# Second attention of a two-layer kernel: keys cut as three tiles of 128 and a rest of 16 instead of four tiles of 100

## The reference, cut to what matters

```
q = (dst @ Wq.T).reshape(B, T_q, H, D_K)          # B 4, T_q 512 here, H 16, D_K 16
k = (src @ Wk.T).reshape(B, T_k, H, D_K)
v = (src @ Wv.T).reshape(B, T_k, H, D_K)
scores = jnp.einsum('bqhd,bkhd->bhqk', q, k)
scores = scores + bias[None]
scores = jnp.where(mask, scores, -1000000000.0)
attn = jax.nn.softmax(scores, axis=-1)
out = jnp.einsum('bhqk,bkhd->bqhd', attn, v).reshape(B, T_q, H * D_K)
return out @ Wo.T
```

## Time and profile before

| | |
|---|---|
| median of 3 runs | 666.35 us |
| profiled execution | 666.83 us, of which the span is 665.0 us |
| TensorE busy | 615.3 us (93%) |
| VectorE / ScalarE / GpSimd busy | 341.1 / 263.4 / 122.0 us |
| chain that ended last | PE 76%, DVE 12%, DMA 4%, issue 3%, ACT 2% |
| mean granted TensorE clock | 0.982 |

### The profile page before, as it was taken

One profiled execution on the slowest core, in us unless ns is written; L12 is line 12 of the kernel. 1 busy time (PEld: TensorE's weight loads), 2 busy tenths in 40 slices (PEclk: granted clock), 3 DMA queues, 4 the chain that ended last, 5 costly groups with the idle time before them and its releaser, 6 DMA issues.

```text
span 665.0 us, 9145 instructions
## 1 busy us (share of the span) xinstructions
PE 615.3 (93%) x3054; PEld 376.6 (57%) x3055; DVE 341.1 (51%) x1089; ACT 263.4 (40%) x364; POOL 122.0 (18%) x178
## 2 busy tenths in 40 slices
PE   3999999999999668799999879999999999999998
PEld 1666666666666435699998433334334333436665
DVE  4264442301303687232232967687887887834301
ACT  0211111111111333334442356776676667683321
POOL 0000000000002000256551036230040040043410
PEclk9999998998989899899999889999999999999999
DMA  9993600811400613253324794252552400041141
GB/s 314 358 366 113 215 1 2 294 61 63 131 0 1 226 54 100 91 139 104 111 71 124 198 155 75 28 86 50 95 86 47 92 1 2 2 131 46 40 135 64
DMA packets 51208, 71.05 MB, mean 107 GB/s; under 512 B 7632, under 2 KB 39802, under 8 KB 50762
## 3 DMA queue, kind: packets, MB, share of 16 engines
q1 hardware_dynamic: 49114, 64.98, 35.7%
q0 software_dynamic: 2048, 5.51, 2.9%
HBM read 48.74 MB, written 15.13 MB: 96 GB/s over the span
## 4 chain that ended last, share of the span: by engine, by line
PE 76%; DVE 12%; DMA 4%; issue 3%; ACT 2%; POOL 1%; DVEq 0%; POOLq 0%; ACTq 0%; SPq 0%
PE ps L955 13%; PE ps L971 13%; PE ps L1536 8%; PE ps L1518 6%; PE ps L1425 6%; PE ps L1143 5%; PE ps L1151 4%; PE ps L1262 4%; PE ps L1274 3%; DVE arena L2265 3%; DVE arena L1976 3%; PE ps L1187 2%; PE ps L1448 2%; PE ps L941 1%; PE ps L1236 1%
## 5 line engine op out<-in xcount | busy, mean ns | idle before, releaser
L1769 ACT ACTIVATE arena<-ps 100x1024 f32<-100x1024 f32 x128 | 123.8, 1020 | 54.7 <-PE ps L1518 54.5
L2265 DVE TENSOR_REDUCE arena<-ps 128x1 f32<-128x400 f32 x256 | 129.5, 563 | 27.7 <-PE ps L1425 25.9
L1576 ACT ACTIVATE arena<-ps 128x512 f32<-128x512 f32 x50 | 29.9, 597 | 172.3 <-PE ps L955 160.5
L955 PE MATMUL ps<-xnT,arena 128*128 128x512 f32 x192 | 94.6, 619 | 0.9 <-DVE xnT L1834 0.9
L971 PEld LDWEIGHTS ps<-arena 128*128 128x128 f32 x384 | 74.1, 194 | 32.2 <-issue 24.3
L971 PE MATMUL ps<-arena 128*128 128x256 f32 x384 | 92.0, 384 | 0.0
L1425 PE MATMUL ps<-arena 97*128 97x400 bf16 x256 | 75.2, 338 | 3.8 <-DMA arena<-arena 1.9
L1518 PE MATMUL ps<-arena 100*100 100x512 bf16 x256 | 76.2, 381 | 1.9 <-DMA arena<-arena 0.7
L1536 PE MATMUL ps<-arena 100*32 100x512 f32 x512 | 69.1, 604 | 0.0
L1425 PEld LDWEIGHTS ps<-arena 97*128 97x128 bf16 x256 | 20.2, 97 | 74.3 <-DVE arena L2265 47.5
L955 PEld LDWEIGHTS ps<-xnT,arena 128*128 128x128 f32 x192 | 37.1, 197 | 29.5 <-issue 27.5
(11 more groups left out here) (247 smaller groups left out, 718.8 us busy)
## 6 DMA issues: line engine op xcount, KB each, us to landing
arena<-in_W SPq DMA_DIRECT2D x16, 512.0 KB, 9.7
arena<-in_ctxT SPq DMA_DIRECT2D x4, 1664.0 KB, 7.4
arena<-in_ctxN SPq DMA_DIRECT2D x4, 1664.0 KB, 12.0
arena<-arena SPq DMA_DIRECT2D x48, 128.0 KB
last_k_parts<-arena SPq DMA_DIRECT2D x24, 100.0 KB, 1.8
arena<-last_k_parts SPq DMA_DIRECT2D x8, 300.0 KB
x_tok<-in_x SPq DMA_DIRECT2D x4, 512.0 KB, 9.3
xn_rows<-xn SPq DMA_DIRECT2D x4, 512.0 KB
```

Source lines behind the costliest of these rows:

```text
L955: ins = pe.matmul(ps[:, 4 + k % 2, :], ctxT_s[:, b % 2, c, f * P:f * P + P], xnT[:, c, S * b:S * b + S], start=(c == 0), stop=(c == KC - 1))
L1576: act.activation(hid[:, k % 4, :], ps[:, 4 + k % 2, :], ACT.Gelu_apprx_tanh).then_inc(s_a, 1)
L1769: act.activation(pexp2[0:KT, c % 4, :, :], ps[0:KT, 2 + 2 * (c % 2):4 + 2 * (c % 2), :], ACT.Exp).then_inc(f_pe, 1)
L2265: dve.tensor_reduce(nm2[:, m // MU % 2, h, j:j + 1], ps[:, FAST.bank(x), 0:KF], AX.X, ALU.max, negate=True).then_inc(s_by["dve"], 1)
```

## The change

- The 400 keys are cut in three tiles of 128 and a rest of 16 keys. Step t = 3 treats the rest: the four heads' scores go as four matmuls with 32 stationary columns each (the last 32 keys, of which the first 16 belong to tile 2) into the four 32-row quarters of one bank. One exponential of 128x512 takes them. Values of the rest are laid out in a tile that is zero outside the block of each head and outside the 16 keys, so that one 128x128 matmul of two instructions adds all four heads' rests.
- A unit has 7 exponentials instead of 8 (`OWN_EXPS`).
- Values of the rest are made by eight matmuls of four strips instead of two; ScalarE copies that piece with one instruction and four small ones, scaled by a column of zeros and ones (`C_REST`). GpSimd prepares the tile with further small instructions. The stored values of batches 2 and 3 have 128 rows instead of 100.
- The maxima products are dealt as 5, 5, 4 and 2 to the four steps (`MAXIMA_IN`), and `LEAD` is 28.
- The turned maxima stand at the beginning of step t = 2, on TensorE ahead of its scores and on ScalarE ahead of its exponentials (`first_of_step`). VectorE's own split for unit 1 moves from step 1 to step 0.

TensorE in one unit without extras, before: L1536 are the values, L1425 maxima products, L1518 scores, L1438 the turned maxima. The piece runs from the values made in the unit's step 0 to the turned maxima in its step 2.

The diff, cut to its core:

```diff
+FULL_T = KF // P
+RK = KF - FULL_T * P
+assert CT == FULL_T + 1 and RK == 16
...
-LEAD = 26
+LEAD = 28
+OWN_EXPS = 2 * FULL_T + 1
+MAXIMA_IN = (0, 5, 10, 14, 16)
...
+    rest = (np.arange(P)[:, None] % VW >= VW - RK).astype(np.float32)
...
+def first_of_step(st):
+    u, t = divmod(st, CT)
+    return [("max rows", u + 1)] if t == 2 and u + 1 < UNITS else []
...
-    if t == 2 and u + 1 < UNITS:
-        found.append(("max rows", u + 1))
...
-def maxima_of_step(st, lo, hi):
-    first = LEAD + HG * st
-    return range(min(first + lo, UNITS * MU), min(first + hi, UNITS * MU))
+def maxima_of_step(st, lo, hi=None):
+    u, t = divmod(st, CT)
+    first, end = LEAD + MU * u + MAXIMA_IN[t], LEAD + MU * u + MAXIMA_IN[t + 1]
+    hi = end if hi is None else first + hi
+    return range(min(first + lo, UNITS * MU), min(hi, UNITS * MU))
+
+
+def exps_from(st):
+
+    u, t = divmod(st, CT)
+    return OWN_EXPS * u + 2 * t
+
+
+def step_of_exp(c):
+    u, r = divmod(c, OWN_EXPS)
+    return CT * u + r // 2
...
     for st in range(STEPS):
+        for name in first_of_step(st):
+            yield name, next(turns), TAKER[name[0]]
         for m in maxima_of_step(st, 0, 2):
             yield ("max", m), next(turns), TAKER["max"]
         for name in extras(st):
             yield name, next(turns), TAKER[name[0]]
-        for m in maxima_of_step(st, 2, HG):
+        for m in maxima_of_step(st, 2):
...
-                            ins = pe.matmul(bank[0:KT, t * D:t * D + D], ctx_e[:, b, k, tt * KT:tt * KT + KT], wv[:, k, :],
-                                            start=(k == 0), stop=(k == KC - 1), skip_group_check=True)
+                        if tt < FULL_T:
+                            for k in range(KC):
+                                ins = pe.matmul(bank[:, t * D:t * D + D], ctx_e[:, b, k, tt * P:tt * P + P], wv[:, k, :],
+                                                start=(k == 0), stop=(k == KC - 1), skip_group_check=True)
+                        else:
+                            for k in range(KC):
+                                for j in range(HG):
+                                    ins = pe.matmul(bank[VW * j:VW * j + VW, t * D:t * D + D], ctx_e[:, b, k, KF - VW:KF], wv[:, k, :],
+                                                    start=(k == 0), stop=(k == KC - 1), skip_group_check=True, tile_position=(0, VW * j))
...
-                assert LEAD == MU + 10
+                assert LEAD == MU + 12
                 queries(2, lambda i: max_products(range(MU + 2 + 2 * i, MU + 4 + 2 * i)))
+                max_products(range(MU + 10, LEAD))
                 pe.wait_ge(s_qf, KC * 2)
...
+                        for x in first_of_step(st):
+                            make(x)
                         for hp in range(HG // 2):
-                            c = 2 * st + hp
-                            if c >= 2:
-                                pe.wait_ge(f_pe, c - 1)
-                            for j in range(2):
-                                h = g * HG + hp * 2 + j
-                                ins = pe.matmul(ps[0:KT, 2 + 2 * (c % 2) + j, :], K2[0:KROWS, b % 2, h, t * KT:t * KT + KT], Q2[0:KROWS, b % 2, h, :],
-                                                start=True, stop=True)
-                            ins.then_inc(s_st, 1)
+                            c = exps_from(st) + hp
+                            if t < FULL_T or hp == 0:
+                                if c >= 2:
+                                    pe.wait_ge(f_pe, c - 1)
+                                for j in range(2) if t < FULL_T else range(HG):
+                                    h = g * HG + hp * 2 + j
+                                    if t < FULL_T:
+                                        ins = pe.matmul(ps[:, 2 + 2 * (c % 2) + j, :], K2[0:KROWS, b % 2, h, t * P:t * P + P], Q2[0:KROWS, b % 2, h, :],
+                                                        start=True, stop=True)
+                                    else:
+                                        ins = pe.matmul(ps[VW * j:VW * j + VW, 2 + 2 * (c % 2), :],
+                                                        K2[0:KROWS, b % 2, h, KF - VW:KF],
+                                                        Q2[0:KROWS, b % 2, h, :], start=True, stop=True, tile_position=(0, VW * j))
+                                ins.then_inc(s_st, 1)
                             max_products(maxima_of_step(st, hp, hp + 1))
                         for x in extras(st):
                             make(x)
                     if st >= 1:
                         i, tv = divmod(st - 1, CT)
                         bv = i // NG
-                        c = 2 * (st - 1)
+                        c = exps_from(st - 1)
                         if tv == 0 and i % NG == 0 and bv >= 2:
                             pe.wait_ge(f_v[bv % 2], 16)
-                        pe.wait_ge(f_pe, c + 2)
+                        pe.wait_ge(f_pe, exps_from(st))
                         if tv == 0 and i >= 1:
                             pe.wait_ge(f_oc, i)
                         if tv == 0 and i == 0:
                             taken(FAST, ("queries", 2, 1))
-                        for j in range(HG):
-                            ins = pe.matmul(ps[VW * j:VW * j + VW, 6, :], V2[0:KT, bv % 2, tv, i % NG * HG + j, :],
-                                            pexp2[0:KT, (c + j // 2) % 4, j % 2, :],
-                                            start=(tv == 0), stop=(tv == CT - 1), tile_position=(0, VW * j))
+                        if tv < FULL_T:
+                            for j in range(HG):
+                                ins = pe.matmul(ps[VW * j:VW * j + VW, 6, :], V2[:, bv % 2, tv, i % NG * HG + j, :],
+                                                pexp2[:, (c + j // 2) % 4, j % 2, :], start=(tv == 0), stop=False, skip_group_check=True,
+                                                tile_position=(0, VW * j))
+                        else:
+                            ins = pe.matmul(ps[:, 6, :], V2[:, bv % 2, tv, i % NG * HG:i % NG * HG + HG, :].rearrange("p h v -> p (h v)"),
+                                            pexp2[:, c % 4, 0, :], start=False, stop=True, skip_group_check=True)
                         ins.then_inc(f_pv, 1)
                     if st < STEPS:
-                        max_products(maxima_of_step(st, 2, HG))
+                        max_products(maxima_of_step(st, 2))
...
-                    act.wait_ge(s_evi, b // 2 + 1)
-                    t = 2 * (u - KC)
-                    act.activation((V2 if b < 2 else vst)[0:KT, b % 2, t:t + 2, :, 0:DK],
-                                   bank[0:KT, :].rearrange("p (t h d) -> p t h d", t=2, d=DK), ACT.Copy).then_inc(s_ev, 1)
+                    act.wait_ge(s_evi, (HG + 1) * (b // 2 + 1))
+                    v = (V2 if b < 2 else vst)[:, b % 2, :, :, 0:DK]
+                    found = bank[:, :].rearrange("p (t h d) -> p t h d", t=2, d=DK)
+                    if u == KC:
+                        ins = act.activation(v[:, 0:2, :, :], found, ACT.Copy)
+                    else:
+                        act.activation(v[:, 2, :, :], found[:, 0, :, :], ACT.Copy)
+                        for j in range(HG):
+                            lo = VW * j
+                            ins = act.activation(v[lo:lo + VW, FULL_T, j:H:HG, :], found[lo:lo + VW, 1, j:H:HG, :], ACT.Copy, scale=cst[lo:lo + VW, C_REST:C_REST + 1])
...
-                    for hp in range(HG // 2):
-                        c = 2 * st + hp
+                    for x in first_of_step(st):
+                        take_max_rows(x[1])
+                    for c in range(exps_from(st), exps_from(st + 1)):
                         act.wait_ge(s_st, c + 1)
                         if c >= 4:
-                            act.wait_ge(f_pv, (c - 4) // 2 + 1)
-                        act.activation(pexp2[0:KT, c % 4, :, :], ps[0:KT, 2 + 2 * (c % 2):4 + 2 * (c % 2), :], ACT.Exp).then_inc(f_pe, 1)
+                            act.wait_ge(f_pv, step_of_exp(c - 4) + 1)
+                        if st % CT < FULL_T:
+                            act.activation(pexp2[:, c % 4, :, :], ps[:, 2 + 2 * (c % 2):4 + 2 * (c % 2), :], ACT.Exp).then_inc(f_pe, 1)
+                        else:
+                            act.activation(pexp2[:, c % 4, 0, :], ps[:, 2 + 2 * (c % 2), :], ACT.Exp).then_inc(f_pe, 1)
                     for x in extras(st):
-                        if x[0] == "max rows":
-                            take_max_rows(x[1])
...
-                    max_steps(maxima_of_step(st, 2, HG))
-                    if t == 1 and 1 <= u + 1 < OWN_SPLITS:
+                    max_steps(maxima_of_step(st, 2))
+                    if t == 0 and 1 <= u + 1 < OWN_SPLITS:
                         split_maxima(u + 1)
...
-            for v in (V2, vst):
-                pool.memset(v[:, :, :, :, DK + 1:], 0.0)
```

(12 more changed lines are left out.)

15 lines of the change are left out of this document (8 added, 7 removed).

## The result

The changed kernel takes a median of 674.11 us (667.79 to 681.64, 11 runs) beside 666.68 us (665.5 to 670.26, 11 runs) of the kernel before, measured together. Two of the changed kernel's executions, 678.03 us and the profiled one, were in a slower state with a lower granted clock, and the ratios in this document leave such executions out: 1.0092 here (95% interval 1.0062 to 1.0123), which is the median of the other nine, 672.84 us, over 666.68. So the change costs 6.2 us by those nine and 7.4 by all eleven. The forecast was 673.8 us, slower.

The account below looks back on a forecast made before the run. TensorE's issue was taken to bound the loop, VectorE two microseconds behind. Units 5.5 + 1.0 + 0.7 + 0.7 + 1.3, tail -2.6 and search +0.9 gave +7.5 on 666.35: 673.8 us, range 657 to 680 (the forecast's own 669 to 680).

Parts of the forecast that it names:

- Work removed: TensorE in a unit: rest's scores 0.45 instead of 0.87, its values 0.87 instead of 1.00, 0.09 less to enter.
- the unit's own issue: TensorE in a unit without extras: 10.40 us, the 11.48 worked out less 1.08 of waits.
- The prices of going into strips and out: TensorE, changing between full-width and strip matmuls: 0.09 us going in and 0.14 going out, explained by a drain.
- one after the other: Rival: the rest's four score matmuls don't overlap in step 3, 0.42 us more per unit, 680 us; chance 0.06.
- Waits added: TensorE waits for banks, 0.54 before step 1's first product and 0.50 before the turned maxima: unit without extras +0.69.
- without waits: Rival: reductions free banks in time, thirteen units take 10.40 instead of 10.79, 659.5 us, 655 without drains; chance 0.16.
- half of them: Rival: waits overlap old ones and strips cost less, +0.2 per unit, about 667 us, 664 without drains; chance 0.20.
- The other units: Loop units walked singly: u4, u8 +1.0; u5, u9 +0.6; u6, u10 +0.5; u7, u11 +0.7; two batches 5.5.
- The tail: u14 and u15, no bank waits and the turned maxima's copy earlier: -2.6 us, of which 1.2 and 1.4.
- The search: Stage before the loop: four small value copies and strip matmuls lengthen the chain, +0.9 us (0.2 to 1.4).
- u0: First of the loop's sixteen units: change 0, as ScalarE is late anyway and two more products are done beforehand.
- The clock: TensorE might lose full clock with a tenth of the loop idle; given nothing of its own, windows showing 1.00.

Follow-up runs that it names:

- half_reduction: Changed kernel, but VectorE's maxima reduction reads only 200 of the 400 columns, leaving out half the keys: 660.29 us, ratio 0.9912.
- keys_only: Kernel before with only the new key tiles: parts 4, 4, 4, 4, lead 26, turned maxima behind step 2's scores, split in step 1: 661.35 us, ratio 0.9920.
- spread: Changed kernel, but in steps 0 and 1 the third maxima product stands ahead of the values, so never three in a row: 668.64 us, ratio 1.0039.
- mask_gpsimd: Changed kernel, but ScalarE copies each value piece in one instruction and GpSimd multiplies the rest's tile by a mask: 673.70 us, ratio 1.0118.
- lead_only: Changed kernel, but four products in each step and turned maxima behind step 2's scores; lead 28 and split in step 0 kept: 663.95 us, ratio 0.9965.
- late_turn: Changed kernel, but turned maxima back behind step 2's scores; parts 5, 5, 4, 2 and lead 28 kept: 668.55 us, ratio 1.0035.
- own_split_late: Changed kernel, but VectorE's split for unit 1 moved back from step 0 to step 1: 676.27 us, ratio 1.0182.
- even_parts: Changed kernel, but parts of 4, 4, 4, 4; turned maxima still first in step 2, lead 28: 669.28 us, ratio 1.0023.
- parts_only: Changed kernel, but lead 26, turned maxima behind step 2's scores and split in step 1; parts 5, 5, 4, 2 kept: 671.31 us, ratio 1.0080.
- tail_early: keys_only with the turned maxima first in step 2 only from u13 on: 662.89 us, ratio 0.9957.
- both: keys_only with turned maxima first from u13 on and GpSimd's mask in place of the four small copies: 662.21 us, ratio 0.9962.
- order_only: Kernel before with its four tiles of 100 and all the rest of the change (parts 5, 5, 4, 2, lead 28, turned maxima first): 683.80 us, ratio 1.0240.

## Why the prediction was right, and where it was not

**Work removed, and the unit's own issue.** 10.40 was worked out, and half_reduction's 10.91 less its 0.5 of waits is 10.4. (The 10.45 of keys_only is another sum: its turned maxima stand directly ahead of the values, where they cost 0.24 and not the 0.42 that they cost ahead of scores, and some 0.3 of small waits is left in it.) The prices of going into strips and out, taken from the earlier trace rows, therefore hold; the rest's scores cost 0.33 to the next product (459.87 to 460.20 in the changed kernel) and 0.09 ahead of them, 0.42 where 0.45 was taken. The rival "one after the other" falls.

**Waits added.** The walk gave 0.54 ahead of step 1's first product, 0.50 ahead of the turned maxima and a unit of 11.48; the trace has both waits in their places, 0.49 each, and 11.40. half_reduction shrinks both; spread takes both away and gets one in another place, as its walk said. The rivals without waits or with half of them fall too. The other units: worked out and measured (us between first scores) u4 13.56 and 13.54, u5 13.5 and 13.48, u6 12.1 and 12.39, u7 13.05 and 12.99. From u1 to u13 the sum is 173.67 against 163.84 before, +9.8, where the prediction had +9.2.

**The tail.** 9.11 and 9.23 for u14 and u15, worked out 9.2 and 9.0: -2.5, predicted -2.6.

**The search.** Predicted +0.9; the trace shows +1.1 in TensorE's wait and +1.2 to the next step of the chain, since the four small copies cost 0.31 each and not 0.2, which is inside the bounds of 0.2 to 1.4. The further 1.7 at the low clock stood in two of ten traces and was not foreseen.

**u0.** Predicted 0, and this step failed. The prediction looked at ScalarE, which is late there, and passed over what the new order does in u0: the turned maxima now stand ahead of scores, and VectorE's split for unit 1, which they need, moves from step 1 to step 0, where GpSimd is still splitting queries. u0 takes 11.97 us before and 12.72 in mask_gpsimd, which has the changed kernel's loop. The windows of u0 in lead_only, late_turn, mask_gpsimd and own_split_late, in this order:

```profile
405.88:417.95 12.07, 10.73 (x65) 3.50 (x64) 10.11 (x21) 8.36 (x10) 5.98 (x7) 1.00 0.32 42
400.73:412.96 12.23, 10.72 (x66) 3.57 (x64) 10.65 (x23) 8.46 (x10) 6.01 (x7) 1.00 0.30 37
402.29:415.01 12.72, 10.99 (x66) 3.61 (x64) 10.83 (x23) 8.56 (x10) 6.01 (x7) 1.00 0.46 61
403.77:417.04 13.27, 10.66 (x66) 3.52 (x64) 9.90 (x23) 8.55 (x10) 5.96 (x7) 1.00 0.44 59
```

The second and the third differ in the place of the turned maxima, +0.49; so do lead_only and even_parts (12.07 and 12.56). The third and the fourth differ in where the split stands, and there the early split is the better one, by 0.55. So of +0.75 about 0.5 is the price of the turned maxima's place, and the move of the split is no loss where they stand first.

In the profiled execution of the changed kernel u0 took 16.18. There the split was longer still. Its four instructions (L2328, 0.17 us from 411.56, is not shown), with GpSimd's beside them:

```profile
409.66 1.16 POOL L2489 TENSOR_TENSOR arena<-arena 128x512 f32<-128x512 f32 x1
409.93 0.33 PE L1456 MATMUL ps<-arena 97*128 97x400 bf16 x1
409.94 0.92 DVE L2326 CAST arena<-arena 128x16 bf16<-128x16 f32 x1
...
410.88 0.61 POOL L2490 CAST arena<-arena 128x512 bf16<-128x512 f32 x1
410.89 0.64 DVE L2327 TENSOR_TENSOR arena<-arena 128x16 f32<-128x16 f32 x1
...
411.57 1.18 POOL L2491 TENSOR_TENSOR arena<-arena 128x512 bf16<-128x512 f32 x1
411.77 1.01 DVE L2329 TENSOR_TENSOR arena<-arena 128x16 bf16<-128x16 f32 x1
412.71 2.49 DVE L2318 TENSOR_REDUCE arena<-ps 128x1 f32<-128x400 f32 x5
413.33 0.82 PE L1456 MATMUL ps<-arena 97*128 97x400 bf16 x2 [1.80 <-DVE arena L2318]
```

Each of VectorE's three instructions that started after a GpSimd instruction ends with it: 410.86 and 410.82, 411.53 and 411.49, 412.78 and 412.75. L2328 started 0.01 us ahead of one and kept its 0.17. Over all fourteen traces the split takes 0.81 to 0.95 us where it stands in step 1 (before, keys_only, own_split_late, parts_only, tail_early, both) and 1.83 to 2.84 where it stands in step 0. The Trainium skill says of the port pair of SBUF that VectorE and GpSimd share that whichever starts first keeps it for its whole instruction while the other blocks; of VectorE it names instructions in a two-port mode, and those with two inputs from SBUF beside a GpSimd instruction that reads SBUF (SBUF — State Buffer, "SBUF: two separate sides"). By this rule a small instruction waits for the rest of a 1.16 us one, and the ends above agree; no run shows the port itself.

Behind the split TensorE waited 1.80 for a bank, 1.03 more than the 0.77 in mask_gpsimd, and from 414.0 to 420.9 it had half its clock. So of u0's +4.2 in this trace, 0.75 comes with the order, and 3.5 with a split of 2.84 instead of 1.84 and the low clock. Only this one execution shows the 3.5, and whether the longer wait brought the low clock is not shown.

**The clock.** It was given no weight, on the ground that every window before has 1.00. In the trace of the changed kernel it is 0.79 in u0 and 0.79 at the search's end, and its runs follow it: 667.79 us at a mean of 0.990, 674.11 at 0.982, 681.64 at 0.972. The low clock and the long split in u0 (3.5) and the low clock in the search (1.7) are 5.2 of the 7.4 us between the trace (+14.8 in the span) and the medians (+7.4).

**The sum.** +7.5 was forecast; +7.4 was measured on the medians of all executions and +6.2 on those behind the ratio. The parts, without what stands in the profiled execution alone, add up to more: +9.8 for u1 to u13, +0.75 for u0, -2.5 for the tail and +1.2 for the search, +9.3. Another measure is mask_gpsimd, whose clock is the one before (0.982) and which does not have the four small copies: its span is 672.2 against 665.0, +7.2, while the loop between the first and the last `turn_values` alone is 7.85 longer. So the direction and the size are right by the largest terms, the units and the tail, each within 0.7. That the total came within 0.1 is luck: every term came out dearer than forecast (the tail's gain smaller), by 1.8 together, and the medians lie 2 to 3 us below the sum of the parts. Where that went stays open. The stages ahead of the loop scatter enough to hide it: the loop's first scores start between 400.73 and 406.41 us in the twelve traces with the new tiles and at 402.26 and 403.28 in the two with the old ones.

## What to carry to other kernels

Where pieces rotate through three buffers, look for runs of three pieces in the written order, and for what the reader of the buffers does just then: the engine averages (8.8 busy of 10.8) said there was slack, and the places in a row decided over half of the loss (5.9 of 10.9 us), and a shorter reduction took away all of it. An instruction that has to wait for another engine belongs behind work that doesn't: the same turned maxima cost next to nothing behind two pairs of scores and 5 to 7 us of the loop in front of them (189.59 against 184.39, 186.12 against 179.48). When a change has a good half and a bad one, run each by itself; here the good half alone, keys_only, was 0.8% faster than the kernel before.

## What the runs showed of the hardware

- Four ScalarE copies of 32x64 took 1.26 us together, 0.31 each, and a copy of 128x256 0.38: a quarter of the rows and columns saves almost nothing, and they don't overlap.
- From the start of a reduction to the start of the product that reuses its bank: 0.60 with 400 columns, 0.39 with 200. A reduction by itself lasts 0.565 and 0.356, so the price of a bank is the reduction's length and some 0.04.
- A small VectorE instruction (128x16, 0.17 to 0.29 alone) that starts during a GpSimd instruction of 128x512 ends with it: it took 0.92, 0.64 and 1.01 us here, and each ended 0.03 to 0.04 after GpSimd's. One that had started 0.01 earlier took 0.17.
- TensorE's clock fell to the lower level after waits of 1.87 (search, two traces of ten), 1.80 and 1.76 us, and also after 1.34 (order_only, u10), 1.18 (even_parts, u12) and 0.80 (order_only, u0). It stayed at the higher one after 2.02 (own_split_late), and in the changed kernel after the same 1.34 (u6) and 1.18 (u12). The wait alone doesn't tell it.
